# A graph attention stage on one Trainium2 core: the order of ScalarE's roots, exponents and normalised rows, and when its function tables are loaded

## The reference, cut to what matters

```python
x = _layernorm(x + _L0_gnn_ref(x, ...), axis=-1)

def _L1_gnn_ref(x, edge_index, weight, attn_l, attn_r):
    xt = jnp.matmul(x, weight).reshape(-1, heads, out_ch)      # 4 heads of 64
    row, col = (edge_index[0], edge_index[1])
    alpha_l = jnp.einsum('ehd,hd->eh', xt[row], attn_l)
    alpha_r = jnp.einsum('ehd,hd->eh', xt[col], attn_r)
    alpha = jax.nn.softmax(jax.nn.leaky_relu(alpha_l + alpha_r, 0.01), axis=1)
    tmp = jnp.einsum('nh,nhd->nd', alpha[:n], xt[col[:n]])
    ...                                                       # tmp repeated over the heads

x = _layernorm(x + _L1_gnn_ref(x, ...), axis=-1)
```

## Time and profile before

| | us |
|---|---|
| median of three runs | 2772.67 (2766.43 to 2774.05) |
| the profiled execution, its own time | 2753.79 |
| its span | 2752.0 |
| VectorE busy, of the span | 1934.5 (70%) |
| TensorE busy, of the span | 1911.2 (69%) |
| GpSimd busy, of the span | 1897.0 (69%) |
| ScalarE busy, of the span | 1570.0 (57%) |

### The profile page before, as it was taken

How to read it: one execution, slowest core, us unless ns; L and a number is a source line. 1 busy time by engine, 2 the same in 40 slices (tenths; PEclk the granted TensorE clock), 3 DMA queues, 4 the chain that set the end, 5 groups by cost and what they waited for, 6 DMA issues and landing times.

```text
span 2752.0 us, 56508 instructions
## 1 busy us (share of the span) xinstructions
PE 1911.2 (69%) x15172; PEld 1459.1 (53%) x15173; DVE 1934.5 (70%) x5868; ACT 1570.0 (57%) x3634; POOL 1897.0 (69%) x1939
## 2 busy tenths in 40 slices
PE   7856677667667667667667767766767763977874
PEld 4444555555555555555555555555555542546773
DVE  5656686686686686686686686686686785845666
ACT  4524566566566566566566566565566564546665
POOL 3277777777777777777777777777777773127772
PEclk9955555565555665555655555555555555979896
DMA  7411111111111111111111111111111114944452
GB/s 210 126 26 35 44 42 34 42 42 34 42 42 34 42 42 34 42 42 34 42 42 34 42 42 34 42 42 34 42 42 34 42 31 150 320 134 140 146 158 83
DMA packets 184030, 183.92 MB, mean 67 GB/s; under 512 B 47738, under 2 KB 150656, under 8 KB 183968
## 3 DMA queue, kind: packets, MB, share of 16 engines
q0 software_dynamic: 63488, 82.04, 12.5%
q1 hardware_dynamic: 120480, 101.12, 11.7%
HBM read 138.76 MB, written 44.26 MB: 67 GB/s over the span
## 4 chain that ended last, share of the span: by engine, by line
POOL 43%; DVE 23%; issue 18%; PE 9%; DMA 4%; ACT 2%; POOLq 0%; DVEq 0%; SPq 0%; ACTq 0%
POOL arena L506 40%; DVE xTb L795 5%; DVE arena L753 5%; DMA arena<-z_table,sidx 2%; DVE arena L884 2%; PE bank L1308 2%; POOL xin L544 2%; PE bank L1054 2%; POOL xTb L546 2%; DVE arena L874 2%; PE bank L1312 1%; ACT arena L1531 1%; PE bank L1043 1%; DVE carry L835 1%; DMA xTb<-x_table,dst 1%
## 5 line engine op out<-in xcount | busy, mean ns | idle before, releaser
L506 POOL DMA_INDIRECT arena<-z_table,sidx x1664 | 1649.9, 992 | 556.2 <-issue 506.9
L1181 PE MATMUL bank<-arena 128*128 x4992 | 557.5, 220 | 92.6 <-DVE xin L761 50.7
L1181 PEld LDWEIGHTS bank<-arena 128*128 128x128 bf16 x4992 | 443.9, 104 | 215.8 <-issue 114.7
L1449 ACT ACTIVATE arena<-bank 128x272 f32<-128x272 f32 x416 | 272.5, 657 | 449.7 <-PE bank L1196 444.9
L761 DVE TENSOR_TENSOR xin<-arena,bank 128x512 f32<-128x512 f32 x208 | 142.5, 685 | 549.2 <-DMA arena<-z_table,sidx 533.1
L1196 PE MATMUL bank<-xto,arena 128*128 128x68 bf16 x4992 | 317.6, 246 | 182.0 <-DVE xto L884 175.9
L1196 PEld LDWEIGHTS bank<-xto,arena 128*128 128x128 bf16 x4992 | 286.0, 132 | 205.8 <-issue 108.8
L1422 ACT ACTIVATE acc<-xTb 128x68 f32 x1632 | 367.9, 309 | 15.8 <-DVE xTb L795 5.6
L1493 ACT ACTIVATE xto<-arena 128x544 bf16<-128x544 f32 x416 | 260.5, 655 | 131.0 <-DVE arena L874 118.3
L1169 PE MATMUL bank<-ident_b,arena 128*128 128x128 bf16 x1664 | 209.9, 305 | 136.2 <-DVE arena L753 136.2
L753 DVE TENSOR_SCALAR arena<-iota_b,didx 128x128 bf16<-128x128 bf16 x1664 | 292.7, 267 | 6.5
(11 more groups left out here) (228 smaller groups left out, 2836.6 us busy)
## 6 DMA issues: line engine op xcount, KB each, us to landing
arena<-z_table,sidx POOLq DMA_INDIRECT x1664, 2.4
xmz_table<-agn SPq DMA_DIRECT2D x49, 256.0 KB
x_table<-arena SPq DMA_DIRECT2D x14, 896.0 KB, 4.5
dspace<-in_x SPq DMA_DIRECT2D x48, 256.0 KB
xin<-in_x SPq DMA_DIRECT2D x13, 896.0 KB, 5.4
arena<-in_x SPq DMA_DIRECT2D x13, 896.0 KB, 11.2
out<-arena SPq DMA_DIRECT2D x13, 896.0 KB, 4.4
xto<-xmz_table SPq DMA_DIRECT2D x6, 896.0 KB, 7.3
```

What stands on the lines that cost most here:

```text
L506: pool.indirect_dma_start(zs[:, h, j, 0:KR], None, z_table, bass.IndirectOffsetOnAxis(ap=sidx[:, h, j:j + 1], axis=0)).then_inc(gathered[h ...
L1181: last = T.matmul(zd_ps[g % 2][:, u * KR:(u + 1) * KR], onehotT[:, g * G + u, :], z3[:, bass.ds(tiles[u], 1), s, :].rearrange("p a c -> p ...
L1449: A.activation(sums[:, :, 1 + q * Q:1 + (q + 1) * Q].rearrange("p c j -> p j c"), sum_ps[q % 2][:, 0:Q * AW].rearrange("p (j c) -> p j c", ...
```

## The change

ScalarE's extra work moves to one place in each round. After the seven copies of group g it now takes, in this order: the root of group g - 1, the exponents of group g itself (before, those of group g - 1, one tile into the next round), and the normalised rows of group g - 1. Two spare instructions (`load_function`) apply Exp and Sqrt to one column of ones, so that the table loads stand at the places written there: Exp after the root, Sqrt right after the exponents. One more loads Exp before the stage begins. VectorE's `norm_bias` of group g - 1 moves from the end of `attend_group(g - 1)` into `attend_group(g)`, between the difference of the logits and the wait for the exponents.

```diff
+        spare_col = sb("spare_col", [P, 2 * NL1 + 1])
...
+            V.memset(spare_col[:, 0:1], 1.0)
...
                 V.tensor_tensor(z, z, spread(lmax[:, 0:m, 0:1], 2, H), ALU.subtract).then_inc(lg_ready, 1)
+                if g >= 1:
+                    norm_bias(1 - h, L1_GROUPS[g - 1][1] - L1_GROUPS[g - 1][0], g - 1, rstd2_ready, nb2_ready)
                 dve.wait_ge(lg_exp, g + 1)
...
                 inverse_variance(h, m, var2_ready)
-                norm_bias(h, m, g, rstd2_ready, nb2_ready)
...
                 attend_group(g, n0, n1)
+            g, (n0, n1) = NL1 - 1, L1_GROUPS[-1]
+            norm_bias(g % 2, n1 - n0, g, rstd2_ready, nb2_ready)
...
+            def load_function(f, column):
+                A.activation(spare_col[:, column:column + 1], spare_col[:, 0:1], f)
+
             def finish_group(g, n0, n1):
-                root(g, g % 2, n1 - n0, var2_ready, rstd2_ready)
                 act.wait_ge(nb2_ready, g + 1)
...
+            load_function(ACT.Exp, 1)
             for n in range(GB - 1):
                 copy_rows_T(n)
             for g, (n0, n1) in enumerate(L1_GROUPS):
...
                     copy_xt(n, g, n0)
-                    if g >= 1 and n == n0:
-                        exp_logits(g - 1, *L1_GROUPS[g - 1])
-                    if g >= 1 and n == n1 - 1:
-                        finish_group(g - 1, *L1_GROUPS[g - 1])
-            exp_logits(NL1 - 1, *L1_GROUPS[-1])
-            finish_group(NL1 - 1, *L1_GROUPS[-1])
+                if g >= 1:
+                    m0, m1 = L1_GROUPS[g - 1]
+                    root(g - 1, (g - 1) % 2, m1 - m0, var2_ready, rstd2_ready)
+                    load_function(ACT.Exp, 2 * g + 1)
+                exp_logits(g, n0, n1)
+                load_function(ACT.Sqrt, 2 * g + 2)
+                if g >= 1:
+                    finish_group(g - 1, m0, m1)
+            root(NL1 - 1, (NL1 - 1) % 2, n1 - n0, var2_ready, rstd2_ready)
+            finish_group(NL1 - 1, n0, n1)
```

## The result

| | before | changed |
|---|---|---|
| median of the runs, us | 2773.36 (2766.43 to 2775.13, 4 runs) | 2742.14 (2732.52 to 2751.22, 4 runs) |
| profiled execution | 2753.79 | 2751.22 |
| its span | 2752.0 | 2749.4 |
| first gather of the attention stage | 2452.1 | 2465.8 |
| from there to the end (the stage) | 299.9 | 283.6 |

The ratio of the runs is 0.9892, 95% interval 0.9863 to 0.9921, or 31 us less. The profiled executions differ by 2.6 us only. Neither can be read alone: in the profiled executions the stage became 16.3 us shorter, and in this one execution of the changed kernel the gathers began 13.7 us later.

A forecast was written before the change was run, and what follows sets the result against it. GpSimd's gathers were taken as the floor, 17.8 us a group against a turn of 18.6, with the gain after they end: 13.75 + 3.93 + 2.16 = 19.8 us, so 2772.67 - 19.8 = 2752.9 us; range 2743 to 2765.

The forecast's parts named there:

- The gathers are the floor: Attention stage: GpSimd's gathers never wait for buffers; 17.8 us a group; copies end at earliest 5.17 us after the needed gather.
- The new wait in front of the leaky relu: VectorE in the attention stage: a new wait of about 3.8 us a group (17.8 - 14.0), released by ScalarE's copies.
- The turn from variance to softmax falls from 5.87 to 1.94 us: From VectorE's reciprocal to its next L982: 5.87 us before, 1.94 after with root, Exp load, spare instruction, exponents and gaps.
- VectorE's own spans don't change: VectorE from L982 to the end of L915: 12.05 us for seven tiles, 7.58 for four, 6.21 for three, unchanged.
- Each group up to 12 begins at its floor: Changed kernel: no group waits beyond the gathers; group 12's last copy at 2695.4 us, its L982 13.75 us earlier.
- the store beside the last gather: Group 11's store, starting at 2702.3 us: landing up to 3.1 us later, last copies still 0.5 us in time.
- The gain of the stage: At the stage's end: 13.75 us in front of group 12, 3.93 in group 13, 2.16 in group 14, together 19.8.
- Rival A: TensorE starves and slows behind ScalarE's 6.9 us piece: turn 18.1 us, gain about 10 us, time 2763; chance 0.14.
- B: Slower: three more tiles a group at half clock, turn 21.5 us, 25 us slower, time 2798; chance 0.04.
- C: The table switch costs twice: ScalarE idle another 1.28 us at the load, gain 16.0 us, time 2757; chance 0.09.
- D: The gathers are no floor: GpSimd speeds up when buffers come free sooner, 55 us gained, time 2718; chance 0.03.
- The time: Whole kernel: 2734.0 us profiled, median 18.9 us above the profiled execution carried over, 2772.67 - 19.8 = 2752.9 us.

The follow-up runs named there:

- after_again: The changed kernel once more, no edit, timed beside the kernel before: 2753.05 us against 2772.03, ratio 0.9933; stage 278.0 us.
- after_half_gather: The changed kernel without the gathers by src, one gather a tile instead of two; executed once for its profile: stage 237.0 us, execution 2721.21 us.
- warm: The changed kernel with 26 spare matmuls ahead of the update stage, second chip: 4449.19 us, ratio 0.9958 to the kernel before.
- before_warm44: The kernel before with 44 spare matmuls ahead of the update stage, second chip: 4456.22 us against 4466.74, ratio 0.9968.
- warm44: The changed kernel with 44 spare matmuls ahead of the update stage, second chip: 4437.12 us, ratio 0.993 to the kernel before.

## Why the prediction was right, step by step

- *The gathers are the floor.* Right on the first chip: 49 us for the change without half of them, 16 to 22 with them, and GpSimd's issues unbroken in both kernels. The new wait in front of the leaky relu, forecast at 3.8 us a group, was 51.4 / 12 = 4.3.
- *The turn from variance to softmax falls from 5.87 to 1.94 us.* Right: 1.90 and 1.89.
- *VectorE's own spans don't change.* Right to 0.03 us each.
- *Each group up to 12 begins at its floor.* For group 12, on which the time hangs, right without stores (+ 0.05) and in after_again (+ 0.5); too hopeful in the first profile (+ 4.2). For the groups before it, it held only without stores: with them most groups of the first profile and five of after_again were 1 to 3 us late, and group 11 4.3 in the first. I had allowed for the store beside the last gather only, with 0.5 us to spare. The landing that cost the time was one in front of group 11's last tiles, and it brought on half clock and a wait for ScalarE after it. The gain of the stage, 19.8 in the forecast, measured 16.3 there, and 21.9 in after_again against the same profile of before, of which 2.2 were quicker gathers.
- *Rival A.* Its parts (TensorE waiting for ScalarE, half clock) do occur, 8.5 us of waits in the changed kernel, but as a consequence of a late landing and not of the long piece. It took 4 of the 20 us once, not 10.
- *B and C*: nothing of either. The twelve turns from group 0 to 12 take 18.2 us in the mean of the first profile and 17.7 in after_again, and no idle time stands about the loads. *D*: not seen. GpSimd's gaps stayed at 0.30 us; its 196 gathers took 247.8 and 246.3 us instead of 248.5, by fewer long ones, and not the 55 us less of this rival.
- *The time.* 2752.9 was predicted; the first four runs gave 2742.14, 0.9 below the range's lower end of 2743 (by the ratio, 0.9892 x 2773.36 = 2743.4, just within it), and twelve more gave 2753.05. That 2753.05 falls on 2752.9 is partly luck: the sum adds a fixed 18.9 us for the median's distance to the profiled execution, and the profiled execution of the kernel before happened to be one whose clock rose early. The runs showed that this distance is no constant but scatter of up to 30 us from run to run, more than the change itself, and that it comes for the most part from the clock's rise in the update stage. Against the kernel before in the same set the change gave 19.0 us where 19.8 were forecast. The range of 22 us should have been wider for that, at its lower end above all.

## What to carry to other kernels

A wait that is removed is worth what the next bound leaves: before adding up waits, compare the turn with the pace of whatever feeds it (18.6 against 17.8 here), and look for the gain after the feed has ended. Where an engine makes two small things that others wait for and one long thing that nobody waits for, the long one goes last. And where runs scatter by more than the effect, find the stage that scatters: 44 spare matmuls narrowed it from 33 us to 7 for the kernel before and 4 for the changed one, and made an effect of 19 us plain in a handful of runs.

## What the runs showed of the hardware

- TensorE's granted clock in a stage in which it was busy throughout rose anywhere between the first few us and about 67 us in, in executions whose kernels are alike up to there (six profiles; 67 is an estimate from the mean of 0.77 between 2400 and 2420 us in after_half_gather, the stage's projections beginning at about 2342). After spare matmuls that ran until the stage began it was high from the first projection in all three kernels profiled with them; after a gap of 4.17 us it was low again.
- With stores of 896 KB beside the indirect gathers the longest landing was 6.5, 5.9 and 4.8 us in three profiles (median 2.8); without the stores it was 4.0 (median 2.7). The gathers' issue kept its pace in all of them.
- On the second chip the same kernel took 4463 instead of 2773 us. What is late there is TensorE and not, as far as the profiles show, the gathers (in warm it takes up the first tile 2.8 us after that tile's second gather begins, against 2.9 for tile 9 on the first chip). Its matmuls come one by one with idle time between them in which it waits for nothing that the profile shows ("issue"). The costliest such line, on the first chip and on the second (page of before, then of before_warm44, the same kernel with spare matmuls; busy us and mean ns, then idle us and what ended most of it):

```profile
L1196 PE MATMUL bank<-xto,arena 128*128 128x68 bf16 x4992 | 317.6, 246 | 182.0 <-DVE xto L884 175.9
```
```profile
L1196 PE MATMUL bank<-xto,arena 128*128 128x68 bf16 x4992 | 427.5, 243 | 1282.5 <-issue 1118.9
```

With L1181 (92.6 us idle on the first chip, 666.7 on the second) that is 1675 of the 1703 us between the two spans. In the attention stage the same happens while group 0 is worked on (timeline of warm44; these are single matmuls of one tile's projection):

```profile
4140.92 0.59 PE L1344 MATMUL bank<-wx,acc 128*128 128x260 f32 x1 [2.42 <-issue]
4143.72 0.59 PE L1344 MATMUL bank<-wx,acc 128*128 128x260 f32 x1 [2.21 <-issue]
```

In none of the six profiles of the first chip does TensorE wait 0.9 us or longer in this way in the attention stage. The copies of group 0 therefore end 33 us behind what was the floor on the first chip, GpSimd runs out of free buffers and waits, once for 5.4 to 6.4 us in every profile, and its gathers take about 281 us instead of 248. The change gave 15 to 16 us of stage there too (354.4 to 339.4, 355.4 to 339.6). Why TensorE pauses like this on this chip stays open.
